# Remainders of two groups of x on GpSimd, small loads on GpSimd's queue, W3 ahead of group 3's x, and the bias products moved inside tiles

## The reference

```python
hidden = concatenate([cond, cond], axis=-1)              # 4 x 512
x_mean = mean(x, axis=1, keepdims=True)                  # 4 x 1 x 512
fused  = concatenate([x, x_mean * ones, hidden * ones])  # 4 x 1024 x 1536
out    = x + relu(einsum("bld,do->blo", fused, W) + b)
```

## Time and profile before

| | |
|---|---|
| time, median of 3 runs (lowest to highest) | 103.92 us (103.63 to 104.15) |
| time of the profiled execution | 103.58 us |
| its span, first to last instruction | 101.8 us |
| busy in the span | PE 96%, DVE 82%, ACT 47%, POOL 38% |
| DMA traffic | 21.41 MB, mean 210 GB/s |

### The profile page before, as it was taken

The page is one execution under the profiler, slowest core; times in us unless marked ns, Lnnn a source line. Parts: engine busy times, 40 slices in busy tenths (PEclk is TensorE's granted clock), DMA queues, the critical chain, the costliest instruction groups (busy, mean ns, idle before and its releaser), DMA issues.

```text
span 101.8 us, 1678 instructions
## 1 busy us (share of the span) xinstructions
PE 97.3 (96%) x523; PEld 78.5 (77%) x523; DVE 83.8 (82%) x161; ACT 48.2 (47%) x118; POOL 38.9 (38%) x35
## 2 busy tenths in 40 slices
PE   5999999999999999999999998999999989999990
PEld 2359999888888788688888885888888858888890
DVE  3165679899899999999999989999998999585671
ACT  3267335966506549879649300964844007300000
POOL 1039600000000000799885504578577529930000
PEclk9999999999999999999999999999999999999999
DMA  1999986999999999999999800591590690699973
GB/s 58 286 294 262 258 200 171 268 238 219 260 332 261 247 243 240 243 243 249 292 356 344 257 2 6 107 266 38 129 265 18 151 251 21 183 245 251 262 284 115
DMA packets 35504, 21.41 MB, mean 210 GB/s; under 512 B 2084, under 2 KB 33192, under 8 KB 35496
## 3 DMA queue, kind: packets, MB, share of 16 engines
q1 hardware_dynamic: 34424, 20.40, 80.8%
q10 hardware_dynamic: 1072, 0.92, 3.1%
HBM read 12.91 MB, written 8.39 MB: 209 GB/s over the span
## 4 chain that ended last, share of the span: by engine, by line
PE 46%; DVE 36%; ACT 8%; issue 6%; DVEq 0%
PE ps_y L504 29%; DVE ps_xt L356 8%; DVE back L369 7%; DVE xl L362 6%; DVE ps_const L390 6%; PE ps_mean L501 6%; ACT xh L279 5%; PE ps_y L624 4%; PE ps_y L622 4%; PE ps_y L623 4%; DVE ps_const L385 3%; DVE w2x L390 2%; DVE bsum L382 2%; ACT relu_t L299 1%; ACT relu_t L286 1%
## 5 line engine op out<-in xcount | busy, mean ns | idle before, releaser
L251 POOL TENSOR_TENSOR xa<-xa,back 128x512 f32 (+1 forms) x26 | 33.5, 1310 | 44.7 <-DVE back L369 44.7
L504 PE MATMUL ps_y<-xh,w1h 128*128 128x512 f32 (+1 forms) x128 | 43.6, 367 | 0.0
L504 PE MATMUL ps_y<-xl,w1h 128*128 128x512 f32 (+1 forms) x128 | 43.0, 363 | 0.0
L504 PE MATMUL ps_y<-xh,w1l 128*128 128x512 f32 (+1 forms) x128 | 42.9, 363 | 0.0
L279 ACT ACTIVATE xh<-ps_xt 128x512 fp32r<-128x512 f32 (+1 forms) x36 | 19.7, 550 | 18.1 <-DVE ps_xt L356 18.0
L504 PEld LDWEIGHTS ps_y<-xh,w1h 128*128 128x128 f32 x128 | 22.6, 188 | 4.9 <-issue 1.2
L356 DVE STREAM_TRANSPOSE ps_xt<-xa 128x512 f32<-128x512 f32 (+1 forms) x36 | 22.3, 642 | 4.9 <-DMA xa<-in_x_dram 4.6
L504 PEld LDWEIGHTS ps_y<-xh,w1l 128*128 128x128 f32 x128 | 22.6, 189 | 3.8
L504 PEld LDWEIGHTS ps_y<-xl,w1h 128*128 128x128 f32 x128 | 22.7, 189 | 3.6
L362 DVE TENSOR_TENSOR xl<-ps_xt,xh 128x512 fp32r<-128x512 f32 (+1 forms) x36 | 22.2, 620 | 3.1 <-ACT xh L279 3.1
L299 ACT ACTIVATE relu_t<-ps_y,bias 128x512 f32<-128x512 f32 x18 | 12.3, 688 | 16.2 <-DVE bias L407 12.7
(11 more groups left out here) (40 smaller groups left out, 45.0 us busy)
## 6 DMA issues: line engine op xcount, KB each, us to landing
xa<-in_x_dram SPq DMA_DIRECT2D x62, 128.0 KB, 4.1
out_dram<-xa SPq DMA_DIRECT2D x28, 256.0 KB, 4.1
w<-in_L_cond_W_dram SPq DMA_DIRECT2D x4, 256.0 KB, 4.7
w<-in_L_cond_W_dram SPq DMA_DIRECT2D x2, 512.0 KB, 6.0
w<-in_x_dram SPq DMA_DIRECT2D x4, 256.0 KB, 5.0
out_dram<-w SPq DMA_DIRECT2D x3, 256.0 KB, 4.0
w<-in_L_cond_W_dram SPq DMA_DIRECT2D x8, 64.0 KB, 3.1
w<-in_L_cond_W_dram ACTq DMA_DIRECT2D x8, 64.0 KB, 3.6
```

What stands on the lines that cost most here:

```text
L251: nc.gpsimd.tensor_tensor(rows, rows, back[:, t], ALU.add).then_inc(added, 1)
L504: return nc.tensor.matmul(ps_y[:, t, ls], lhs, rhs, start=start, stop=stop, skip_group_check=True)
```

## The change

1. GpSimd makes the remainders of groups 2 and 3 (`POOL_GROUPS`). Since GpSimd can't read PSUM here, VectorE turns these eight pieces into the four places of `back`, ScalarE reads them there, and GpSimd subtracts, with a semaphore of its own (`pool_xl_ready`). The first four turn-backs wait until all eight are done.
2. The four DMAs of `cond` and the four of b go from SP's queue to GpSimd's: `cond` at its start, b behind the remainders of W1.
3. SP issues W3 ahead of group 3's x.
4. `const_product` and all `mean_bias` stand inside tiles (`MEAN_AT`): the first two in tile (2,0) ahead of k = 1, the others in (2,2) ahead of k = 2, (4,2) ahead of k = 2 and (6,1) ahead of k = 2.
5. On ScalarE the later `x_high` are placed by `rounded_after`: four to three relus from n = 8 on, where one stood behind each relu before.
6. On VectorE `mean_terms(2)` and `(3)` stand at the end of n = 11 and n = 19, and `sum_bias` 1, 2 and 3 ahead of `turn_back` 2, 13 and 24 (before: 4, 13 and 22). `mean_terms` now waits for the `x_high` of its groups.

```diff
+    POOL_GROUPS = range(H, SLOTS)
+    def rounded_after(n):
+        return RELU_RING + 3 * (n - pieces_to(SLOTS)) // NK
+    MEAN_AT = {(H, 0, 1): 0, (H, 2, 2): 1, (2 * H, 2, 2): 2, (3 * H, 1, 2): 3}
...
+        def turned_x(n):
+            g, _l, nl, _k = pieces[n]
+            return turned[:, pool_place(n)] if g in POOL_GROUPS else ps_xt[:, bank(n), 0:nl]
...
             load_x(sp, 1, ORDER)
-            sp.wait_ge(cond_zeroed, 1)
-            for j in range(NQ):
-                sp.dma_start(cond_c[Q * j:Q * j + B], cv[j].rearrange("b (m k) -> b m k", k=CK)).then_inc(cond_landed, 16)
             load_x(sp, 2, ORDER)
             load_w2(sp, ORDER)
-            for j in range(NQ):
-                sp.dma_start(b_row[Q * j:Q * j + Q], bvec[P * j:P * j + P].partition_broadcast(Q)).then_inc(b_landed, 16)
-            load_x(sp, 3, ORDER)
             for r in range(2):
                 sp.dma_start(w3[:, r], w3v[r]).then_inc(w3_landed, 16)
+            load_x(sp, 3, ORDER)
...
             nc.gpsimd.memset(cond_c[:], 0.0).then_inc(cond_zeroed, 1)
+            pool.wait_ge(cond_zeroed, 1)
+            for j in range(NQ):
+                pool.dma_start(cond_c[Q * j:Q * j + B], cv[j].rearrange("b (m k) -> b m k", k=CK)).then_inc(cond_landed, 16)
...
+            for j in range(NQ):
+                pool.dma_start(b_row[Q * j:Q * j + Q], bvec[P * j:P * j + P].partition_broadcast(Q)).then_inc(b_landed, 16)
+
+            for n in range(pieces_to(H), pieces_to(SLOTS)):
+                g, _l, _nl, k = pieces[n]
+                pool.wait_ge(xh_ready, n + 1)
+                nc.gpsimd.tensor_tensor(xl[:, g % SLOTS, k], turned[:, pool_place(n)], xh[:, g % SLOTS, k],
+                                        ALU.subtract).then_inc(pool_xl_ready, 1)
...
-                for _n in range(steps_of_x(n, 2)):
+                while n_x < len(pieces) and rounded_after(n_x) == n:
                     x_high(n_x)
                     n_x += 1
...
                 dve.wait_ge(relu_done, n + 1)
                 if n >= BACK_RING:
                     dve.wait_ge(added, n + 1 - BACK_RING)
+                else:
+                    dve.wait_ge(pool_xl_ready, NK * len(POOL_GROUPS))
...
+                    if (g, t, k) in MEAN_AT:
+                        b = MEAN_AT[g, t, k]
+                        if b == 0:
+                            const_product()
+                        else:
+                            pe.wait_ge(bias_ready, b)
+                        mean_bias(b)
```

More of the change, by code:

```diff
@@ L159, in build @@
         last_hi_ready, last_hl_ready = sem("last_hi_ready"), sem("last_hl_ready")
+        turned = back[:].rearrange("p r lb m -> p r (lb m)")
+        def turned_x(n):
+            g, _l, nl, _k = pieces[n]
+            return turned[:, pool_place(n)] if g in POOL_GROUPS else ps_xt[:, bank(n), 0:nl]
         def load_x0(eng, half, quadrants):
@@ L312, in _ @@
             save(3)
-            n_x = pieces_to(H)
-            x_high(n_x)
-            x_high(n_x + 1)
+            for n in range(pieces_to(H), pieces_to(H + 1)):
+                x_high(n)
             save(NK)
-            x_high(n_x + 2)
-            x_high(n_x + 3)
             save(NK + 1)
             save(NK + 2)
-            n_x += NK
+            n_x = pieces_to(H + 1)
             x_high(n_x)
@@ L326, in _ @@
             x_high(n_x + 3)
-            n_x += NK
-            assert n_x == pieces_to(SLOTS) and SAVED == 2 * NK + 2
+            n_x = pieces_to(SLOTS)
             for n in range(len(tiles)):
@@ L334, in _ @@
                 relu(n)
-                for _n in range(steps_of_x(n, 2)):
+                while n_x < len(pieces) and rounded_after(n_x) == n:
                     x_high(n_x)
                     n_x += 1
+            assert n_x == len(pieces) and SAVED == 2 * NK + 2
             act.wait_ge(rows_set, 2)
@@ L479, in _ @@
                     n_x += 1
+                if n // NK + SLOTS - 1 < G and n // NK > 0 and n // NK % H == 0 and n % NK == NK - 1:
+                    mean_terms(n // NK // H + 1)
             dve.wait_ge(last_bias_landed, 16)
@@ L528, in mean_bias, with const_product @@
                 last.then_inc(mean_done, 1)
+            def const_product():
+                pe.wait_ge(cond_spread, 1)
+                pe.wait_ge(w2x_step, NK)
+                pe.wait_ge(w3_landed, 16 * 2)
+                for r in range(2):
+                    for k in range(CK):
+                        for j in range(NQ):
+                            last = nc.tensor.matmul(ps_const[Q * j:Q * j + Q, 0:P], cond_t[:, k], w3[:, r, k, P * j:P * j + P],
+                                                    start=(r == 0 and k == 0), stop=(r == 1 and k == CK - 1))
+                last.then_inc(const_summed, 1)
             def group0_low(half, k):
@@ L578, in _ @@
                 tile(1, 1, t)
-            def const_product():
-                pe.wait_ge(cond_spread, 1)
-                pe.wait_ge(w2x_step, NK)
-                pe.wait_ge(w3_landed, 16 * 2)
-                for r in range(2):
-                    for k in range(CK):
-                        for j in range(NQ):
-                            last = nc.tensor.matmul(ps_const[Q * j:Q * j + Q, 0:P], cond_t[:, k], w3[:, r, k, P * j:P * j + P],
-                                                    start=(r == 0 and k == 0), stop=(r == 1 and k == CK - 1))
-                last.then_inc(const_summed, 1)
-            for t in range(NK):
-                pe.wait_ge(y_saved, NK + t + 1)
-                for k in range(NK):
-                    if t == 0:
-                        pe.wait_ge(xl_ready, pieces_to(H) + k + 1)
-                    elif t == 1 and k == NK // 2:
-                        const_product()
-                        mean_bias(0)
-                    last = product(H % SLOTS, k, t)
-                last.then_inc(y_ready, 1)
-            pe.wait_ge(bias_ready, 1)
-            mean_bias(1)
-            for g in range(H + 1, LAST):
+            for g in range(H, LAST):
                 for t in range(NK):
@@ L614, in _ @@
                     tile(g, g % SLOTS, t)
-                    if g % H == 0 and g < LAST - 1 and t == 2:
-                        pe.wait_ge(bias_ready, g // H)
-                        mean_bias(g // H)
             def last_product(y, k, r, cols_h, cols_l, start, stop):
```

58 lines of the change are left out of this document (30 added, 28 removed).

## The result

| | before | after |
|---|---|---|
| time, median | 103.6 us (103.49 to 104.15, 6 runs) | 106.84 us (105.37 to 108.54, 6 runs) |
| ratio, 95% interval | | 1.026 (1.019 to 1.033) |
| profiled execution, its span | 103.58, 101.8 | 106.56, 104.8 |

The forecast was 103.6, with a range of 102.8 to 104.7. The kernel became slower and the time lies outside the range. The ratio is taken from the fast executions alone, four of the six of after, and comes to 2.7 us, while the medians, over all executions, lie 3.2 apart.

A forecast was written before the change was run, and what follows sets the result against it. TensorE, 96% busy, was taken as the bound, standing still some 0.85 us, with VectorE late. 0.85 gained, 0.3 (mean_bias(1)) and 0.2 (tile (4,3)) given back: 0.35 less than the 103.92 median, 103.6; range 102.8 to 104.7.

The forecast's parts named there:

- L: Time at which the last piece of group 3's x has landed; 30.3 taken, range 29.3 to 31.2.
- the sum: Landing of group 3's x, added up from group 1's last landing through group 2, W2, W3 and x: 30.7.
- the freed issuing: SP, rid of cond and b, gives up 1.37 and 1.82 of issuing and reaches the later loads that much earlier.
- The price of L: TensorE's new wait at mean_bias(1) is L - 30.05: 0.3 at 30.3, nothing at 29.3, 1.2 at 31.2.
- x after 31: Rival: group 3's x lands late, mean_bias(1) waits 1.5 at L = 31.5, time 104.9; chance 0.12.
- The old waits: TensorE's waits for VectorE's mean_terms at mean_bias(2) and (3) go: gain 0.85.
- Tile (4,3): TensorE waits 0.2 there for relu(15), now behind two x_high of group 6; between nothing and 0.4.
- The remainders on GpSimd: Eight x_low leave VectorE for GpSimd at 1.26 each; nothing on the path unless each took over 0.2 more.
- cond and b on GpSimd's queue: Cost put at nothing: cond's DMAs may take 1.59 each before w1l is late, b's have room for 2.5 each.
- The const product: On TensorE at 30.1, with W3 at 26.4 and mean_terms(0) at 28: no wait, cost 1.42 as before.

The follow-up runs named there:

- relu15_first: The changed kernel with relu(15) on ScalarE ahead of the two x_high of group 6 that stood before it; 106.5 us in two runs (104.7 and 108.31).
- w3_behind: The changed kernel with W3 again behind group 3's x, const product in tile (2,1) and mean_bias(1) in (2,3); 105.97 us, ratio 1.023.
- all_places: The kernel before with all of the change but cond and b on GpSimd's queue and W3 ahead of group 3's x; 105.23 us, ratio 1.013.
- w3_pool: The changed kernel with W3's two DMAs moved from SP's queue to GpSimd's, behind b; 105.55 us in two runs.
- w3_fine: The changed kernel with W3 loaded in 8 DMAs of 32 partitions instead of 2 of 128; 106.21 us, runs from 104.92 to 108.78.
- rounding_only: pool_only with ScalarE's order of the change, so that relu(15) stands behind two x_high; 106.96 us, ratio 1.031.
- pool_only: The kernel before with part 1 of the change alone, the remainders of groups 2 and 3 on GpSimd; 102.88 us, ratio 0.9937.
- order_only: The kernel before with only W3 moved ahead of group 3's x; 107.34 us, ratio 1.033.

## Why the prediction was wrong, by its own steps

- **L is the step that failed.** Forecast 30.7 by the sum, 30.3 taken, 29.3 to 31.2 as bounds; measured 33.4, and 34.0 and 31.6 in the two other kernels with the same loads. From last landing to last landing the trace of after has 6.1 for group 2 (4.3 taken), 4.5 for W2 (4.1), 3.7 for W3 (3.2) and 4.1 for x (4.3), from 15.0 instead of 14.8: the greatest miss is group 2. Two things make up the 2.7 between sum and result. The pace was taken too fast: from group 1's 112th mark to group 3's it is 16.8 (14.2 to 30.9), where the sum has 15.9. And the sum let the lag of the last mark stay as it is at group 1, 0.8; at groups 2 and 3 it is 2.4. I had let the freed issuing close a gap. Of group 2 it brought 112 marks forward by 0.8 (18.65 against 19.42), but the last came at 21.1, after the 20.4 of before. And I took less than my own sum, at the pace of the best seven pieces, where the last of eight is what counts. (Two small slips in the working, 103.05 for 103.07 and 0.49 a piece for 0.50, change nothing.)
- **The price of L was right.** L - 30.05 gives 3.35 at L = 33.4; 2.97 were measured, with TensorE itself 0.5 later at that place (38.2 instead of 37.7). In relu15_first it gives 1.5, and 1.37 were measured. The rival "x after 31" is what happened: with L = 33.4 it gives 103.92 - 0.85 + 3.35 + 0.3 = 106.7, against 106.84. It had a chance of 0.12 and a price for L = 31.5 only. The early loss of 0.4 does not add to it: TensorE comes to the wait that much later and waits that much less.
- **The old waits went, as forecast.** `mean_terms(2)` ended at 62.51, where L + 28.8 = 62.2, and 1.0 ahead of TensorE (1.3 forecast). That does not hang on the size of the stall: behind a wait at `mean_bias(1)` both engines count from L, and in relu15_first, with L = 31.6, the terms are 1.0 early too (60.74 against 61.73). With W3 behind x (w3_behind, all_places), which the forecast did not have to treat, the same place waits 0.91, for there it is the const product that holds VectorE.
- **Tile (4,3):** 0.2 forecast, 0.33 measured, and 0.34 and 0.32 in w3_pool and w3_fine. With W3 behind x it is 1.02 of waiting in w3_behind and all_places, and 3.26 in rounding_only.
- **The remainders on GpSimd** cost nothing, as forecast: eight at 1.29, ScalarE reads SBUF at 0.62 instead of 0.60, and pool_only is faster by 0.6%.
- **cond and b on GpSimd's queue** were put at nothing. GpSimd was held 0.55 for each DMA of `cond`, well under the 1.59 that the step allowed, and `w1l` did not wait for it; the price is another, 0.5 to 0.6, along with W1's later landing. The step looked at the engine that issues and not at the loads beside which these transfers, now ten microseconds earlier, run.
- **The const product** did not wait (30.29 to 30.61), as forecast.

So the change holds a contradiction: with W3 ahead, x is late and TensorE waits at `mean_bias(1)`; with W3 behind, the const product is late and the tighter places wait. By the ratios W3's move alone costs 3.3% (order_only), the rest with W3 behind 2.3% (w3_behind), 1.3% without the queue's move (all_places), and the whole change 2.6%. The prices do not add up, since in either order VectorE stands still once in about the same stretch: 3.99 for x in after, 3.00 for the const product in w3_behind.

## What to carry to other kernels

When loads already fill the DMA engines, as here, moving one ahead delays the one behind it, and issuing earlier buys little: read when the last part of a load is there, not the pace of the middle ones, and allow for a scatter of that last part. Moving work off a busy engine was the part that paid. W3's place, the queue, the products' places and ScalarE's order each cost 0.6 us or more where they were tried alone; VectorE's order was not. So take the parts of such a change one at a time. A price worked out for one order of the loads must be worked out again for another, since another transfer may then hold the same engine.
